# Second mixture of experts: a third PSUM bank for its first products in some chunks, its second products and the addition to the residual later in the plan

## The reference, cut to what matters

```python
x = x + 0.5 * _L2_ffn_ref(_layernorm(x), ...)
x = x + _L2_attn_ref(_layernorm(x), ...)          # a mamba layer with scans
x = x + 0.5 * _L2_ffn_ref(_layernorm(x), ...)

def _moe_forward(x, router_w, w1, w2, shared_gate_up, shared_down, shared_gate_w):
    probs = softmax(x @ router_w)
    topw, topi = top_k(probs, 2)
    combine = zeros((n, 8)).at[arange(n)[:, None], topi].add(topw)
    h = silu(einsum('nd,edf->nef', x, w1))         # 8 experts, 128 x 128 each
    ye = einsum('nef,efd->ned', h, w2)
    routed = einsum('ne,ned->nd', combine, ye)
    gu = x @ shared_gate_up
    shared = silu(gu[:, :128]) * gu[:, 128:] @ shared_down
    shared = sigmoid(x @ shared_gate_w) * shared
    return routed + shared
```

## Time and profile before

| | |
|---|---|
| median of three runs | 3355.2 us |
| the three runs | 3356.87, 3344.37, 3355.2 us |
| profiled execution | 3346.75 us |
| its span, first to last instruction | 3345.0 us |
| mean granted TensorE clock | 0.961 |
| TensorE (PE) busy | 2973.2 us, 89% |
| weight loads (PEld), beside PE | 1851.0 us, 55% |
| VectorE (DVE) busy | 2390.9 us, 71% |
| ScalarE (ACT) busy | 2002.1 us, 60% |
| GpSimd (POOL) busy | 882.7 us, 26% |

### The profile page before, as it was taken

The page is one execution under the profiler, slowest core; times in us unless marked ns, Lnnn a source line. Parts: engine busy times, 40 slices in busy tenths (PEclk is TensorE's granted clock), DMA queues, the critical chain, the costliest instruction groups (busy, mean ns, idle before and its releaser), DMA issues. The chain is left out here.

```text
span 3345.0 us, 43971 instructions
## 1 busy us (share of the span) xinstructions
PE 2973.2 (89%) x14254; PEld 1851.0 (55%) x14254; DVE 2390.9 (71%) x5307; ACT 2002.1 (60%) x3426; POOL 882.7 (26%) x971
## 2 busy tenths in 40 slices
PE   7998899898999998899887777888999998899998
PEld 5776333233777663356553333355677766677776
DVE  5666788785554776777766878867777777577776
ACT  4443667677444446744346766544577775377786
POOL 1020433422000001210003776710133332033332
PEclk9999999999999999999998888899999999799999
DMA  2000122210100330023333222224311010001111
GB/s 89 1 15 25 57 62 66 77 62 33 36 1 0 116 100 13 1 87 99 102 114 106 89 76 89 80 80 139 99 36 48 29 51 4 22 27 51 45 32 54
DMA packets 117868, 193.37 MB, mean 58 GB/s; under 512 B 18396, under 2 KB 31132, under 8 KB 117512
## 3 DMA queue, kind: packets, MB, share of 16 engines
q1 hardware_dynamic: 116056, 187.68, 17.6%
q10 hardware_dynamic: 1584, 2.88, 0.2%
HBM read 172.23 MB, written 18.25 MB: 57 GB/s over the span
## 5 line engine op out<-in xcount | busy, mean ns | idle before, releaser
L420 POOL TENSOR_TENSOR norm_rstd<-norm_rstd,minus_half 128x4 f32<-128x4 f32 (+1 forms) x136 | 176.6, 1299 | 1187.4 <-DVE norm_rstd L407 1176.9
L2532 ACT ACTIVATE main_tiles_r<-banks,feature_cols 128x512 fp32r<-128x512 f32 x512 | 353.1, 690 | 187.5 <-PE banks L262 165.9
L2540 DVE TENSOR_TENSOR main_tiles_r<-main_tiles,main_tiles_r 128x512 fp32r<-128x512 f32 x512 | 383.5, 765 | 68.0 <-ACT main_tiles L2533 66.2
L986 DVE TENSOR_REDUCE gate_scratch<-banks 128x2 f32<-128x1024 f32 (+2 forms) x320 | 345.0, 1114 | 90.1 <-PE banks L251 60.6
L1146 ACT ACTIVATE main_tiles<-banks 128x512 f32<-128x512 f32 (+1 forms) x608 | 314.5, 581 | 127.1 <-PE banks L1127 85.6
L260 PE MATMUL banks<-normed_pairs,moe_weights 128*128 128x512 f32 x740 | 368.2, 498 | 13.3 <-ACT main_tiles L2533 6.4
L2577 POOL TENSOR_TENSOR normed<-normed,main_tiles 128x512 f32<-128x512 f32 x128 | 217.9, 1702 | 532.8 <-DVE main_tiles L2566 532.8
L2533 ACT ACTIVATE main_tiles<-banks,feature_cols 128x512 f32<-128x512 f32 x512 | 349.9, 683 | 0.0
L260 PE MATMUL banks<-main_tiles_r,moe_weights 128*128 128x512 f32 x700 | 308.9, 441 | 31.9 <-DVE main_tiles_r L2540 26.9
L262 PE MATMUL banks<-normed_pairs,moe_weights 128*128 128x512 f32 x740 | 292.0, 395 | 0.0
L261 PE MATMUL banks<-normed_pairs,moe_weights 128*128 128x512 f32 x740 | 291.7, 394 | 0.0
(11 more groups left out here) (374 smaller groups left out, 6672.2 us busy)
## 6 DMA issues: line engine op xcount, KB each, us to landing
main_tiles<-gates_d SPq DMA_DIRECT2D x400, 256.0 KB, 3.2
mamba_tiles<-c_rows_d SPq DMA_DIRECT2D x92, 256.0 KB, 3.3
spare_nat<-c_rows_d SPq DMA_DIRECT2D x36, 256.0 KB, 3.4
found_d<-main_tiles SPq DMA_DIRECT2D x32, 256.0 KB, 2.0
parts_d<-bf_parts SPq DMA_DIRECT2D x48, 128.0 KB, 1.8
q_stacks<-parts_d SPq DMA_DIRECT2D x192, 32.0 KB
k_stacks<-parts_d SPq DMA_DIRECT2D x192, 32.0 KB
weight_staging<-in_w SPq DMA_DIRECT2D x22, 256.0 KB, 3.8
```

The lines of the kernel that those rows point to most:

```text
L420: eng.tensor_tensor(rstd[:, k, 1, 0:w], rstd[:, k, 0, 0:w], minus_half[:, 0:w], ALU.pow).then_inc(s.norm_pow)
L986: eng.tensor_reduce(o.rearrange("p (n s) -> p s n", s=2)[:, :, j0:j0 + per], psum[:, b0:b0 + 2, 0:per * (k1 - k0)].rearrange("p s (n c) -> ...
L2532: eng.activation(pair_3(j)[0], psum[:, 2 + j % 2, :], ACT.Relu, bias=bias)
L2540: eng.tensor_tensor(lo, h3_of(j), hi.bitcast(F32), ALU.subtract).then_inc(s.m3_lo)
```

## The change

There are three edits.

The banks of the first products are now worked out by a small planner, `m2_first_bank`, which takes the bank whose last use is longest ago. In chunks 1 to 4 and 11 to 15 it may use a third bank, 6, which no other stage has then; in the other chunks it has banks 2 and 3 as before. `m2_free` gives the wait that belongs to the last use.

The second products are planned 1.2 us later (6.2 in place of 5.0), and the addition to x too (8.8 in place of 7.6).

Two stages outside get other waits: `pe_fold`, which uses bank 6 from chunk 5 on, also waits for silu 45 of the mixture, and the first two products of the fourth layer both wait for the last silu and for the last up product.

```diff
--- before.py
+++ after.py
@@ -1975,34 +1975,58 @@
             for e in range(9):
                 yield 9 * cc + e, cc, e, begin + M2_US * e + after + (shared if e == 8 else 0.0)
 
+
+
+    m2_bank, m2_before, m2_used = {}, {}, {2: -2, 3: -1}
+
+    def m2_first_bank(cc):
+
+        if cc in (1, 11):
+            m2_used[6] = -1
+        elif cc in (5, 8):
+            m2_used.pop(6, None)
+        for e in range(10):
+            bank = min(m2_used, key=m2_used.get)
+            m2_bank[cc, e] = bank
+            last = m2_used[bank]
+            m2_before[cc, e] = None if last < 80 * (cc // NC_) else \
+                (s.m2_up, last // 10 + 1) if last % 10 == 9 else (s.m2_h, 9 * (last // 10) + last % 10 + 1)
+            m2_used[bank] = 10 * cc + e
+
+    for cc_ in range(2 * NC_):
+        m2_first_bank(cc_)
+    assert [m2_bank[NC_ - 1, e] for e in (8, 9)] == [2, 3]
+
+    def m2_free(eng, cc, e):
+
+        bank = m2_bank[cc, e]
+        if m2_before[cc, e] is not None:
+            eng.wait_ge(*m2_before[cc, e])
+        elif cc < NC_:
+            eng.wait_ge(*{2: (s.m1_h1, 127), 3: (s.m1_h1, 128), 6: (s.m1_done, 16)}[bank])
+        elif bank == 2:
+            eng.wait_ge(s.m2_h, 72)
+            eng.wait_ge(*mb_dve(7, "yd"))
+        elif bank == 3:
+            eng.wait_ge(s.m2_up, 8)
+            eng.wait_ge(s.st_h, NS * NC_)
+        else:
+            eng.wait_ge(*mb_misc_end(6))
+
     def pe_m2_first(eng):
         for k, cc, e, when in m2_items(0.0):
-            z = 10 * cc + e
             yield when
             if e == 0:
                 eng.wait_ge(*paired(("m2", cc)))
             if k == 0:
                 eng.wait_ge(s.wl_lo, w2_count)
-            if z < 2:
-                eng.wait_ge(s.m1_h1, 127 + z)
-            elif k == 72:
-                eng.wait_ge(s.m2_h, 72)
-                eng.wait_ge(*mb_dve(7, "yd"))
-            elif k == 73:
-                eng.wait_ge(s.m2_up, 8)
-                eng.wait_ge(s.st_h, NS * NC_)
-            elif e == 1:
-                eng.wait_ge(s.m2_up, cc)
-            elif e == 0:
-                eng.wait_ge(s.m2_h, k)
-            else:
-                eng.wait_ge(s.m2_h, k - 1)
+            m2_free(eng, cc, e)
             hi, lo = pair_of(("m2", cc))
-            split_mm(eng, psum[:, 2 + z % 2, :], parts(w2r, e * P), hi, lo, True, True).then_inc(s.m2_z1)
+            split_mm(eng, psum[:, m2_bank[cc, e], :], parts(w2r, e * P), hi, lo, True, True).then_inc(s.m2_z1)
             if e == 8:
                 yield when + 0.8
-                eng.wait_ge(s.m2_h, k)
-                split_mm(eng, psum[:, 3, :], parts(w2r, (E8 + 1) * P), hi, lo, True, True).then_inc(s.m2_z1)
+                m2_free(eng, cc, 9)
+                split_mm(eng, psum[:, m2_bank[cc, 9], :], parts(w2r, (E8 + 1) * P), hi, lo, True, True).then_inc(s.m2_z1)
 
     def act_m2_first(eng):
         for k, cc, e, when in m2_items(1.0):
@@ -2013,7 +2037,7 @@
                 eng.wait_ge(s.m1_lo1, 125 + k)
             else:
                 eng.wait_ge(s.m2_wt, k - 3)
-            eng.activation(h1_of(k), psum[:, 2 + z % 2, :], ACT.Silu).then_inc(s.m2_h)
+            eng.activation(h1_of(k), psum[:, m2_bank[cc, e], :], ACT.Silu).then_inc(s.m2_h)
 
     def dve_m2_weighed(eng):
         for k, cc, e, when in m2_items(2.4):
@@ -2023,7 +2047,7 @@
             if e == 8:
                 yield when + 0.8
                 eng.wait_ge(s.m2_z1, 10 * cc + 10)
-                eng.tensor_tensor(h1_of(k), psum[:, 3, :], h1_of(k), ALU.mult).then_inc(s.m2_up)
+                eng.tensor_tensor(h1_of(k), psum[:, m2_bank[cc, 9], :], h1_of(k), ALU.mult).then_inc(s.m2_up)
                 yield when + 2.0
                 eng.wait_ge(s.m2_up, cc + 1)
             eng.wait_ge(*gate_ready(u))
@@ -2044,7 +2068,7 @@
         return 5 - cc % 2, (s.m2_done, cc - 1)
 
     def pe_m2_second(eng):
-        for k, cc, e, when in m2_items(5.0, 1.0):
+        for k, cc, e, when in m2_items(6.2, 1.0):
             yield when
             if e == 0:
                 eng.wait_ge(*m2_acc(cc)[1])
@@ -2055,7 +2079,7 @@
 
     def dve_m2_x(eng):
         for cc, begin in enumerate(m2_at):
-            yield begin + M2_US * 8 + 7.6
+            yield begin + M2_US * 8 + 8.8
             xs = chunk(cc % NC_)
             eng.wait_ge(s.m2_z2, 9 * (cc + 1))
             eng.tensor_tensor(xs, psum[:, m2_acc(cc)[0], :], xs, ALU.add).then_inc(s.m2_done)
@@ -2434,6 +2458,7 @@
     def pe_fold(eng):
         yield T_MB + 2.0
         eng.wait_ge(s.m1_done, 16)
+        eng.wait_ge(s.m2_h, 45)
         eng.wait_ge(s.nat_in, 48)
         for o in range(4):
             w = N2["f1"] + o * P
@@ -2505,9 +2530,8 @@
                 eng.wait_ge(*paired(("m3", cc)))
             if cc == 0 and f == 0:
                 eng.wait_ge(s.wl_lo, w3_base + 2 * (e + 1))
-            if j == 0:
+            if j < 2:
                 eng.wait_ge(s.m2_h, 144)
-            elif j == 1:
                 eng.wait_ge(s.m2_up, 16)
             else:
                 eng.wait_ge(s.m3_h, j - 1)
```

## The result

The changed kernel took 3357.89 us (median of 12 runs, 3352.51 to 3363.61), the kernel before 3346.62 (12 runs, 3341.49 to 3356.87): 1.0029 of before, 95% interval 1.0021 to 1.0038. That is some 10 us more, and within the 0.5% that the prediction called no change. The forecast was 3362 in 3346 to 3376, worked out as +11.0 us.

The account below looks back on a forecast made before the run. It took a loop through several engines, none full, to bound the kernel; 8.8 + 1.0 - 1.3 + 2.2 + 0.7 - 1.0 + 0.6 = +11.0 us, added to 3350.8, gave 3362, range 3346 to 3376.

Parts of the forecast that it names:

- The turn of 20.5 us: Chunk loop: transpose to router's end 8.59, to first weighing 4.13, to transpose 7.80; sum 20.52 us, the whole chunk.
- The third bank at 0: First products wait for the evacuation three places back, not two: put at 0, between -0.4 us and 0 a chunk.
- One stop of 3.3 us ahead of the transpose: TensorE's two stops ahead of the gate transpose become one of 3.3 us, 3.6 if the third bank gives its tenths.
- Two falls in three chunks at 2.2 each: TensorE's clock falls behind the single stop in chunks 1 to 5 and 14: +8.8 us, bounds 0 and +19.
- Rival 2: No more clock falls than now, small terms alone, +0.5: 3351 us; supported by clock 1.00 in 1669.40:1672.58; chance 0.24.
- -0.12 a chunk: Later x addition on VectorE hides a gap: 0.12 us off its 7.80, -1.3 us in 11 chunks with this loop.
- The +1.1 in chunks 6 and 10: One-bank chunks: the first second product waits for the later x addition, 1.1 us goes through; +2.2 (0 to +2.2).
- +0.7 in chunk 11: The x addition's wait puts two TensorE stops close together: +0.7 us for a clock fall (0 to 1.6).
- Chunks 12 to 14: Chunks 12 and 13: two stops become one of 4 us, +0.5 each; chunk 14 counted with the clock falls of chunks 1 to 5.
- The end of chunk 7, -1.0: L389 stands one second product earlier, so the mamba layer's scans start sooner: -1.0 us, 1.19 at most.
- The start of the fourth layer's stage, +0.6: At L2532 ScalarE's wait for the last second product, moved behind one more first product: +0.6 us (0 to +1.2).
- Rival 3: The waits are what bounds: 1.07 + 1.09 us vanish in ten chunks, -22: 3329 us; chance 0.10.

Follow-up runs that it names:

- the run with the stop filled: Changed kernel plus two unused matmuls ahead of the gate transpose in chunks 1 to 5 and 11 to 14, against the kernel before: 3349.4 us, ratio 1.0003.

## Why the prediction was right, and where it wasn't

The time and its sign came out as forecast, 10 us against 11, and for the cause named, the clock: the run with the stop filled shows it. Where in the kernel the clock would fall, and what would make it fall, came out only in part, and that the sum came so near is in part luck. By its steps:

- The turn of 20.5 us holds. Without falls the changed chunk takes 20.3 to 20.4, the forecast 20.4. Both runs that alter the turn shorten the chunk.
- The third bank at 0: right.
- One stop of 3.3 us ahead of the transpose: right, 3.31. Two falls in three chunks at 2.2 each: in chunks 1 to 5 there were two falls where the term counts 3.3, costing 2.5 and 1.3 us, 3.8 where it has 7.3. So the term is mis-sized, mainly by the count. The repeated run had three there. The third fall, in chunk 6, came by the wait for the addition and cost 2.0 with it.
- That the single stop is what makes the clock fall failed as a rule. The addition alone gave three falls with the stop split, and the second products alone gave none in three of five chunks with stops of 3.28 us. Stops alike to 0.01 us fall or don't, and not in the same chunks when the same kernel runs again. What decides between them was not found. Rival 2's row, two stops with work between at clock 1.00, was no safe ground either.
- The addition: -0.12 a chunk was right to 0.1. The +1.1 in chunks 6 and 10 isn't there: chunk 6 grew by 0.4 where the clock stayed, chunk 10 became 0.3 shorter. But its effect on the clock is put at +0.7 in chunk 11 alone (it was 0.4, by the stop ahead of S0), and this is most of what it did. The forecast hangs its main term on the second products; by themselves they cost nothing in the time of the whole kernel (0.9991), and the addition alone gave 1.0017.
- Chunks 12 to 14: wrong. The prediction took the order of chunk 2 for all. S2 stays ahead of the transpose there, so no single stop formed, and from the transpose of chunk 11 to that of chunk 14 the changed kernel takes 66.3 us where the kernel before took 68.4. From the first scan input to the fourth layer's stage the sum is +1.4 us, where the terms of chunks 8 to 15 and of that stage's start made +4.3 (1.5 + 1.0 - 0.6 + 1.1 + 0.7 + 0.6).
- The end of chunk 7, -1.0: it was -0.56. The start of the fourth layer's stage, +0.6: the wait grew by 0.4.
- Rival 3, that the waits themselves are what bounds: out. The changed kernel has no wait ahead of S2 any more and is slower; the stop only moved. The Trainium skill's reading of a repeated gap as a lack of PSUM (Perfetto Trace Analysis, Optimization Strategy) isn't borne out either, by the run with the third bank alone.

Chunks 0 to 7 were forecast at +6.7 and made +5.5, the rest at +4.3 and made +2.2 with the end of the program; the other +2.3 arose nearly all ahead of the stage, in code that the change doesn't touch. So the sum came nearer to the forecast than its parts did. The 3362 itself is 4 us over the measured 3357.9, since it was added to 3350.8, where the kernel before then took 3346.6.

## What to carry to other kernels

Close the turn first: name the instructions through which a period returns to itself, add them up, and see whether they make the period. An instruction that waits in an in-order queue should stand behind the work that doesn't need it; that gave 0.2 to 0.3% here, while a bank more gave nothing that could be measured. A later place in the plan can cost more through the clock than it gives by the order, and filling a stop with useless work is a cheap test of it. Profile the same kernel twice before you explain why one chunk falls and another doesn't. And compare the order of every chunk, not of one: two planned times that tie are settled by rounding.

## What the runs showed of the hardware

Idle stretches of the same 3.31 us with no work in them left TensorE's clock at 2.4 GHz in one chunk and took it to 1.2 GHz in another. Two stops of 1.27 and 1.09 us with one second product between them had a fall behind them in two chunks of the kernel with the addition alone later and none in three others. A stop of 1.96 us ahead of S0 in chunk 6 had a fall behind it in the changed kernel, and one of 1.95 us none in the kernel with the stop filled. At 1.2 GHz the second product takes 2.08 us and at 2.4 GHz 1.02.
